# Edge chunks in the first attention: one a tile over tiles 12 to 28 in place of two over tiles 12 to 21, and the slots' decode and turn at the attention's end

## What is computed

```python
attn = einsum('nhqd,nhkd->nhqk', q, k) * scale
attn = softmax(attn + bias[None], axis=-1)
out = einsum('nhqk,nhkd->nhqd', attn, v) @ w_proj + b_proj
...
e = leaky_relu(a_src[src] + a_dst[dst], negative_slope=0.2)
ee = exp(e - segment_max(e, dst)[dst])
alpha = ee / (segment_sum(ee, dst)[dst] + 1e-16)
agg = segment_sum(h[src] * alpha[:, :, None], dst)
```

## Time and profile before

| | |
|---|---|
| median of 3 runs | 825.82 us (824.45 to 827.58) |
| the profiled execution: its own time | 827.57 us |
| the profiled execution: its span | 825.8 us |
| mean granted clock of TensorE over the span | 0.698 of full |
| busy over the span | PE 558.9, PEld 335.6, DVE 559.2, ACT 319.0, POOL 276.7 us |

### The profile page before, as it was taken

One profiled execution on the slowest core, in us unless ns is written; L12 is line 12 of the kernel. 1 busy time (PEld: TensorE's weight loads), 2 busy tenths in 40 slices (PEclk: granted clock), 3 DMA queues, 4 the chain that ended last, 5 costly groups with the idle time before them and its releaser, 6 DMA issues. The chain is left out here.

```text
span 825.8 us, 12352 instructions
## 1 busy us (share of the span) xinstructions
PE 558.9 (68%) x4215; PEld 335.6 (41%) x4215; DVE 559.2 (68%) x1298; ACT 319.0 (39%) x725; POOL 276.7 (34%) x341
## 2 busy tenths in 40 slices
PE   5607857698999572466681587519667744889886
PEld 4404535366665471222230343209645532423222
DVE  6994997999855665899986696573523448366452
ACT  1116436354578321233442244120143433555443
POOL 6003112021222106777776777000031101134334
PEclk9997558568899555555555655555569965599898
DMA  6100000000000014111111110000000000000001
GB/s 189 32 0 1 2 1 1 1 2 1 2 1 3 1 14 73 23 27 33 37 37 21 22 38 8 2 0 1 1 0 1 1 1 0 1 2 0 13 13 26
DMA packets 28632, 13.04 MB, mean 16 GB/s; under 512 B 22080, under 2 KB 25761, under 8 KB 28322
## 3 DMA queue, kind: packets, MB, share of 16 engines
q1 hardware_dynamic: 23842, 10.82, 5.2%
q0 software_dynamic: 4736, 1.51, 2.1%
HBM read 10.77 MB, written 1.54 MB: 15 GB/s over the span
## 5 line engine op out<-in xcount | busy, mean ns | idle before, releaser
L1436 POOL DMA_INDIRECT edge_scratch<-src_rows_dram,slot_src_index x144 | 150.8, 1047 | 46.3 <-issue 43.1
L594 POOL TENSOR_TENSOR wa_kbd<-wa_qk,headmask 128x512 f32<-128x512 f32 x32 | 34.9, 1091 | 161.5 <-ACT wa_qk L704 161.5
L491 POOL TENSOR_TENSOR ln_xs<-xn,ln_stats 128x256 f32<-128x256 f32 x32 | 19.4, 614 | 155.9 <-DVE ln_stats L459 93.9
L723 ACT ACTIVATE wa_probs<-wa_scores,wa_max 128x64 f32<-128x64 f32 x256 | 64.4, 334 | 9.0 <-DVE wa_max L771 8.9
L544 PE MATMUL ln_pT<-ident,ln_xs 128*64 128x128 f32 (+1 forms) x112 | 27.4, 403 | 49.6 <-POOL ln_xs L491 48.7
L1566 PE MATMUL moe_h_ps<-xT,moe_w 65*128 65x512 f32 x64 | 58.9, 1074 | 0.3 <-ACT list_onehots L1496 0.3
L1986 DVE SCALAR_TENSOR_TENSOR moe_weighted<-moe_y_ps,moe_b_cols,moe_G 128x512 f32<-128x512 f32 x32 | 24.0, 751 | 46.8 <-ACT moe_G L1959 44.7
L2045 POOL TENSOR_TENSOR moe_acc<-moe_acc,moe_weighted 128x512 f32<-128x512 f32 x28 | 37.8, 1350 | 49.7 <-DVE moe_weighted L1986 49.6
L1558 PE MATMUL edge_acc<-edge_scratch 128*64 128x64 bf16 x672 | 23.0, 237 | 45.4 <-DVE edge_scratch L115 45.4
L1945 ACT ACTIVATE moe_hidden<-moe_h_ps,moe_b_cols 128x1024 f32<-128x1024 f32 x32 | 35.6, 1114 | 40.7 <-PE moe_h_ps L1877 40.7
L634 PE MATMUL wa_s_ps<-wa_kbd,wa_qk 64*64 64x512 f32 x128 | 47.4, 826 | 3.5 <-issue 2.7
(11 more groups left out here) (394 smaller groups left out, 1351.7 us busy)
## 6 DMA issues: line engine op xcount, KB each, us to landing
edge_onehot_T<-slot_lo_dram SPq DMA_DIRECT2D x16, 288.0 KB, 3.3
edge_scratch<-src_rows_dram,slot_src_index POOLq DMA_INDIRECT x144, 2.5
edge_scratch<-in_L_ffn_edge_index SPq DMA_DIRECT2D x2, 1024.0 KB, 6.2
xrow<-in_x SPq DMA_DIRECT2D x4, 256.0 KB, 7.6
out_h<-h SPq DMA_DIRECT2D x4, 256.0 KB, 2.6
moe_w<-in_L_ffn_W SPq DMA_DIRECT2D x3, 256.0 KB
src_rows_dram<-src_rows SPq DMA_DIRECT2D x1, 320.0 KB
moe_w<-in_L_ffn_W SPq DMA_DIRECT2D x2, 128.0 KB
```

Of the source, the lines that this page charges most:

```text
L594: pool.tensor_tensor(kbd[b][:], bc_at(qk[b][:, 1, :], 1, NH), bc(k.headmask[:, 0, :], WIN), ALU.mult).then_inc(kbd_ready, 1)
L723: ins = act.activation(pr[b][:, h, :], sc[b][:, h, :], ACT.Exp, bias=mx[b][:, h:h + 1], scale=-1.0)
L1436: pool.indirect_dma_start(gs[b][:, j, :], None, srow_dram, bass.IndirectOffsetOnAxis(edges.src_index[:, x:x + 1], axis=0))\
```

## The change

`MOVES` becomes a list of chunks by step, from step 12: two, then one in each of seven, two, one in each of seven, two. So TensorE multiplies two chunks in steps 12, 20 and 28 and one in each of the others from 13 to 27. `STEP_OF[j]` is the step in which chunk j is multiplied. VectorE builds chunk j two steps ahead (`AHEAD`), or when the ring has room: chunks 0 and 1 in step 10, one in each of steps 11 to 17, chunks 9 and 10 in step 18, one in each of steps 19 to 25, chunks 18 and 19 in step 26. `TURN_STEP` goes from 23 to 29: there VectorE decodes. The transposes follow at the end of TensorE's step 31, the last, where they stand ahead of the turn and the projection of the last output. The copies out of the bank are taken after VectorE's last addition, by one more turn of the generator, and SP's stores follow them. The amount of work is the same.

```diff
-PREFIX_STEP, MOVE_STEP, MOVES, RING = 7, 12, 2, 6
-TURN_STEP = MOVE_STEP + FOUND_CHUNKS // MOVES + 1
+PREFIX_STEP, MOVE_STEP, RING, AHEAD = 7, 12, 6, 2
+MOVES = [2, 1, 1, 1, 1, 1, 1, 1, 2, 1, 1, 1, 1, 1, 1, 1, 2]
+STEP_OF = [MOVE_STEP + s for s, moves in enumerate(MOVES) for _ in range(moves)]
+assert len(STEP_OF) == FOUND_CHUNKS
+TURN_STEP = STEP_OF[-1] + 1
...
                 if c + 2 < n:
                     bias(c + 2, b, False)
             add(n - 1, 1)
+            edges.now = n
+            next(lists)
...
         for j in range(FOUND_CHUNKS):
-            assert self.now < MOVE_STEP + j // MOVES, (j, self.now)
+            assert self.now < STEP_OF[j], (j, self.now)
             wide = RCH * (reach(j)[1] - reach(j)[0]) // 2
-            while self.now <= MOVE_STEP + (j - RING) // MOVES:
+            while self.now < STEP_OF[j] - AHEAD or j >= RING and self.now <= STEP_OF[j - RING]:
                 yield
             if j >= RING:
                 dve.wait_ge(self.moved, j - RING + 1)
...
-        while self.now < TURN_STEP + 4:
+        while self.now < TILES:
             yield
         turned = self.bank[:, 0:2 * P].rearrange("p (x q) -> p x q", x=2)
         dve.wait_ge(self.turned, 1)
...
-        if MOVE_STEP <= c < MOVE_STEP + FOUND_CHUNKS // MOVES:
-            for j in range(MOVES * (c - MOVE_STEP), MOVES * (c - MOVE_STEP + 1)):
+        for j in range(FOUND_CHUNKS):
+            if STEP_OF[j] == c:
                 low, high = reach(j)
                 pe.wait_ge(self.move_ready, 3 * (j + 1))
```

## The result

The changed kernel takes **821.23 us** (median of 8 executions, 814.42 to 828.3), the kernel before 825.81 beside it (8, 823.31 to 833.99). The ratio is 0.9899, with a 95% interval of 0.9857 to 0.9941: **faster by 1.0%**, about twice what was to be told from no change. Forecast were 823.5 us and "no change"; the time lies within the range, the sign had been given 0.31. Executions of one kernel lie 10 to 28 us apart, and a ratio compares the undisturbed ones alone, so it is not exactly that of the medians.

What follows compares the result with a forecast made beforehand. TensorE bounds tiles 20 to 29, while VectorE, building two chunks a tile, holds it up over tiles 11 to 19. Terms: -4.4 stretch, -0.5 tile 13, +2.6 end, sum -2.3 us, forecast 823.5 us, range 817.5 to 829.

Steps and rivals of the forecast that it cites:

- the stretch: TensorE's turn of tile 14 to that of tile 30: 77.5 us instead of 81.87, a gain of 4.4.
- the decode's stand in tile 24: Decode's delay of TensorE in the kernel before, tile 24: taken at 1.30 us, with no fall of the clock.
- Tiles 10 to 13: Ahead of the stretch: 0.5 us gained in tile 13, nothing in tiles 10 to 12.
- The end: Behind tile 28: decode 0.7, transposes 0.5, copies 0.5 and SP's stores 0.87, together 2.6 us lost.
- Tile 18: VectorE builds chunks 9 and 10 there, 7.1 us against 4.5: a TensorE stand of 2.6 us.
- One fall at 2.2: TensorE's clock falls once, behind the stand of tile 18, and costs 2.2 us.
- Tiles 16 and 17: VectorE's lag, from meeting GpSimd's operation, makes TensorE stand some 0.3 us in each.
- Tile 26's double: VectorE builds chunks 18 and 19 there, 5.8 us against 4.3: a stand of 1.5 us.
- The slack being in use: At tile 26, the lag TensorE doesn't feel, about 1.5 us, was taken as already used up.
- Even flow: Rival: TensorE at 2.4 GHz from tile 13 to 30 with hardly a stand, stretch gain 10.7, 817 us; chance 0.31.
- The thin multiplies: Rival: one chunk a tile leaves the clock at 1.2 GHz four tiles longer after a fall, 832 us; chance 0.13.

Runs made afterwards that it cites:

- e_end_early: Changed kernel with the two transposes in step 30 and the copies in step 31: 827.69 us against 828.84 for the kernel before (1.001).
- e_stand24: Changed kernel plus nine spare VectorE operations of the decode's width ahead of chunk 15: 828.26 us against 825.94 for the kernel before (1.0066).
- b3: Kernel before, unchanged, profiled once more: 83.66 us from TensorE's turn of tile 14 to that of tile 30.
- first: First profiled execution of the changed kernel, no further edit: 828.30 us, with 78.66 us from turn 14 to turn 30.
- a2: Changed kernel, unchanged, second repetition: 823.9 us against 828.84 for the kernel before (0.9985).
- a_again: Changed kernel, unchanged, first repetition: 824.4 us against 833.06 for the kernel before (0.9946).
- e_best2: Changed kernel, doubles only in tiles 12 to 14, transposes in tile 30, copies in 31, no list step behind the last addition: 815.73 us against 825.94 (0.9871).
- The end alone: Kernel before's moves, two a tile, with the changed decode and end; two runs: 828.45 us against 833.06 (0.9987), 827.29 against 825.94 (1.0013).
- e_nodouble: Changed kernel with two chunks in each of tiles 12 to 14, one in each of 15 to 28: 822.58 us against 833.06 for the kernel before (0.9906).
- e_best1: Changed kernel with doubles only in tiles 12 to 14, transposes in tile 30, copies in 31: 822.99 us against 828.84 for the kernel before (0.9954).

## Why the forecast was wrong

**What failed is the term of the sum for the stretch, "a gain of 4.4": its base.** It set 77.5 us for the changed kernel against the 81.87 of one execution. The first holds nearly (77.2 to 78.7, mean with e_end_early 77.9). The second does not stand for the kernel: its four executions average 83.8, so the term measured 5.9. The working had the decode's stand in tile 24 at its length, 1.30 us, because in the earlier trace rows the clock stayed at 1.00 over tiles 20 to 30, "so gaps of about 0.3 a tile did it no harm". In two executions of four the clock fell in or right behind tile 24, which made tiles 25 to 28 6.8 and 3.5 us longer, 2.6 us on the mean of the four. Without these falls the term would have measured 3.3, less than the 4.4: the forecast had the rest a little too high and this fall at nothing. That the stand is behind it is borne out by e_stand24 (a stand and a fall, with multiplies around) and by the two executions with the moves of before and no stand there (no fall); but these are few, in b3 only the first 0.43 us of the stand had passed, and four executions do not give the share of such ones. A single profile showed the cheap face.

**Tiles 10 to 13** were the second, smaller miss: 0.5 in tile 13 and nothing before. Where the clock rises at the same place as before (first, a2 and e_stand24: 30.96 to 31.01 against 31.78) the gain is 0.8; over the executions it averages 1.4. That the rise comes earlier with the changed moves is not shown, since the kernel before varied by 1.5 there too. The prediction read from its one execution that the rise came only after the first edge multiplies; in a_again it came ahead of them.

**The end** was right in kind and near in size. Copies and stores: 1.69 - 0.32 = 1.37, as 0.5 + 0.87 had been taken, and SP is in the stage's meeting. The transposes cost 0.22 instead of 0.5 (from the reciprocal to the last addition 2.31 us, before 2.09). The decode cost 0.52 instead of 0.7 (turn 30 to turn 31 in 4.14 us, before 3.62). Sum 2.1 against 2.6; e_best2 takes 1.6 of it back and so shows the price.

With these the sum is -5.9 - 1.4 + 2.1 = -5.2 us in place of -2.3. Within the late rise alone it is -3.2 - 0.8 + 2.1 = -1.9, close to the forecast and under the 4.1 that can be told; within the early one -8.6 - 1.9 + 2.1 = -8.4. The three ratios make 8.3, 4.5 and 1.2. The end alone fits the mean of the four just so: its stretch averages 79.4, 4.4 under the 83.8; from turn 30 to the next stage it takes 3.1 us more than before (12.64 and 9.58), so that it should have been some 1.3 us faster, and the second of its ratios leaves room for 1.3 at most. So the direction is shown, and that the stretch of the kernel before is on the mean dearer than in the one profile; the size hangs on how many executions of each course a set holds, and how much of it is the falls of tile 24 in the medians stays open. Of the stages behind no part could be assigned to the change: from the next stage to the end the kernel before took 548.1 to 551.8 us and the changed one 545.9 to 549.4, which is spread of the same size as the gain; e_nodouble, with the same end, took 553.4.

**The stands.** Tile 18: 2.6 forecast, 3.10 in two executions and about 1.0 in the two others. One fall at 2.2: half speed cost up to 3.1 in each, in one fall in the first and a2, in two shorter ones in the others. Tiles 16 and 17: 0.70 and none, for 0.3 each. Tile 26's double, 1.5 forecast, made no stand: 0.25 to 0.30 idle as in its neighbours. "The slack being in use" was wrong there: with lists of 2.0 to 2.7 us VectorE had caught up, and waited for TensorE itself in steps 20 and 21 (0.79 + 1.05 and 0.32 + 1.20 us). That the sum came out near 77.5 is partly two errors that cancel.

**The rivals.** Even flow has its stretch in e_best2, 71.43 us (and 0.53 for chunk 3 ahead of it) where the rival had 81.87 - 10.7 = 71.2; the changed kernel did not reach it, because of tile 18. The thin multiplies did not leave the clock low: behind the fall in tile 19 TensorE was at full clock by 222.95, ahead of the two chunks of step 20 and with one chunk in each step since 13. The Trainium skill (TensorE: Matmul & The Clock Gate, section "What's actually happening") takes half rate as the default that activity lifts. The windows of e_best2 at 1.00 over 71.43 us agree; the 22.58 busy microseconds at a mean of 0.54 in the earlier trace rows do not.

Open is what decides a fall. TensorE stood 0.68 to 0.69 us in tile 18 in e_nodouble, e_best1 and e_best2 alike, and the clock fell there in the first two and not in the third. Open is also how often each face of a kernel comes: four executions are too few for a share.

## What to carry to other kernels

Where a stage is bound by an engine whose granted clock falls in some executions and not in others, a short stand is not priced at its length: profile the kernel several times, compare executions of like course, and take the mean of the stretch, not one execution, as the base of a sum. Spread side work in equal pieces, without a double step in the middle, and put work that must leave the critical engine's way where another wait already stands (here 1.6 us came back by taking copies and stores one step earlier). When a piece of a generator moves, look what the next turn of it will take.

## What the runs showed of the hardware

- The granted clock of TensorE can differ between executions of one kernel in work that nothing changed: tiles 6 to 9 took 27.7 to 28.0 us in some and 31.1 to 31.2 in others, of either kernel. That alone is 3.2 us, three quarters of what can be told from no change.
- The decode's delay in tile 24, with the same instructions around it, came with no low clock in two executions, with 10.2 us of it in one and with 17.0 in another (3.5 and 6.8 us on the next four tiles); and behind a stand of 0.69 us the clock fell in e_nodouble, while behind one of 0.68 it held in e_best2.
- The stage's end waits for SP's program: the next stage began 0.44 us after SP's second DMA was issued. It did not wait for the data: the profile's DMA issues give that store 1.4 us to landing, which from 276.18 is behind the next stage's beginning at 277.04.
